# One language-model layer: norm chains in another order, values 68 columns wide, moments from the accumulator, gates by Tanh

## The reference, cut to what matters

```python
h = _L0_tok_ref(weight, x, end_ids)
h = h + attn(_layernorm(h))           # 8 heads of 16
#   xn = layernorm(input);  Q, K: one number per head;  V = xn @ Wv per head
#   P = softmax(-(Q - K)**2 / 4);  O = P @ V;  head_result @ Wm + input
h = h + ffn(_layernorm(h))            # 8 experts, 2 chosen per row
#   hh = layernorm(input) * g + b;  logits = hh @ w_r.T + b_r
#   topk_vals, topk_idx = top_k(logits, 2);  gates = softmax(topk_vals)
#   hid = gelu(hh @ W1[e] + b1[e]);  out = sum gate * (hid @ W2[e] + b2[e])
#   return input + out
```

## Time and profile before

| | us |
|---|---|
| median of three runs | 105.89 |
| the runs | 105.89, 107.15, 105.58 |
| profiled execution, its own time | 105.69 |
| its span, first to last instruction | 104.0 |
| busy in the span: PE, DVE, ACT, POOL | 85.4, 58.5, 55.4, 32.5 |

### The profile page before, as it was taken

How to read it: one execution, slowest core, us unless ns; L and a number is a source line. 1 busy time by engine, 2 the same in 40 slices (tenths; PEclk the granted TensorE clock), 3 DMA queues, 4 the chain that set the end, 5 groups by cost and what they waited for, 6 DMA issues and landing times.

```text
span 104.0 us, 1441 instructions
## 1 busy us (share of the span) xinstructions
PE 85.4 (82%) x435; PEld 67.6 (65%) x435; DVE 58.5 (56%) x174; ACT 55.4 (53%) x120; POOL 32.5 (31%) x65
## 2 busy tenths in 40 slices
PE   0081998499699995379999999999999999989940
PEld 0051437467499983369777777777777776779940
DVE  0998569688989555628809113404041329259870
ACT  0757814689998412213934564645556563118750
POOL 6963130039999624400000005415050505000000
PEclk9999999999999999955569999999999999999999
DMA  0589999090000000000000000000000000003774
GB/s 5 67 294 403 323 290 276 21 378 28 0 9 0 0 0 0 0 0 0 0 0 0 6 0 0 0 0 0 0 0 0 6 0 0 0 3 106 297 275 129
DMA packets 8168, 7.59 MB, mean 73 GB/s; under 512 B 1441, under 2 KB 6241, under 8 KB 8033
## 3 DMA queue, kind: packets, MB, share of 16 engines
q1 hardware_dynamic: 7440, 7.41, 22.5%
q10 hardware_dynamic: 720, 0.10, 0.6%
HBM read 5.40 MB, written 2.11 MB: 72 GB/s over the span
## 4 chain that ended last, share of the span: by engine, by line
PE 70%; DVE 15%; ACT 4%; issue 4%; DMA 3%; POOL 1%; DVEq 0%
PE ps L1214 20%; PE ps L1133 8%; PE ps L1299 7%; PE ps L1203 6%; PE ps L1204 6%; PE ps L1205 5%; PE ps L1047 4%; PE ps L1092 3%; DMA ends_i<-in_end_ids 3%; DVE closest L842 2%; PE ps L1226 1%; ACT hn_t L573 1%; PE ps L1107 1%; PE ps L1118 1%; ACT L638 1%
## 5 line engine op out<-in xcount | busy, mean ns | idle before, releaser
L657 ACT ACTIVATE w_f<-ps,ffn_cols 128x384 f32<-128x384 f32 x32 | 18.2, 580 | 15.9 <-PE ps L1205 15.9
L1214 PE MATMUL ps<-w_f 128*128 128x384 f32 x64 | 26.0, 496 | 0.0
L1203 PE MATMUL ps<-hn_hi,w_hi 128*128 128x384 f32 (+2 forms) x35 | 21.4, 613 | 1.4 <-DVE hn_lo L888 1.2
L513 POOL TENSOR_TENSOR acc<-acc,term 128x384 f32<-128x384 f32 x6 | 8.6, 1439 | 34.3 <-DVE term L973 34.3
L973 DVE SCALAR_TENSOR_TENSOR term<-ps,ffn_cols,gate_bc 128x384 f32<-128x384 f32 (+2 forms) x9 | 5.1, 571 | 22.8 <-PE ps L1214 15.9
L1204 PE MATMUL ps<-hn_lo,w_hi 128*128 128x384 f32 (+2 forms) x35 | 12.8, 366 | 0.0
L1205 PE MATMUL ps<-hn_hi,w_lo 128*128 128x384 f32 (+2 forms) x35 | 12.7, 364 | 0.0
L1214 PEld LDWEIGHTS ps<-w_f 128*128 128x128 f32 x64 | 11.8, 193 | 0.9
L1203 PEld LDWEIGHTS ps<-hn_hi,w_hi 128*128 128x128 f32 x35 | 7.8, 222 | 5.8 <-DVE hn_lo L888 1.3
L1204 PEld LDWEIGHTS ps<-hn_lo,w_hi 128*128 128x128 f32 x35 | 7.9, 227 | 3.8 <-issue 0.3
L461 POOL TENSOR_TENSOR w_lo<-w_f,w_hi 128x512 fp32r<-128x512 f32 x8 | 10.0, 1276 | 0.0
(11 more groups left out here) (185 smaller groups left out, 134.1 us busy)
## 6 DMA issues: line engine op xcount, KB each, us to landing
w_f<-in_w SPq DMA_DIRECT2D x4, 512.0 KB, 7.0
w_f<-in_w SPq DMA_DIRECT2D x8, 256.0 KB, 6.9
out_y<-w_f SPq DMA_DIRECT2D x6, 256.0 KB, 2.6
cls_all<-cls_dram SPq DMA_DIRECT2D x1, 1024.0 KB, 4.3
out_y<-w_f SPq DMA_DIRECT2D x4, 128.0 KB, 2.3
wm_sb<-in_wm ACTq DMA_DIRECT2D x1, 64.0 KB, 2.4
emb<-in_weight SPq DMA_DIRECT2D x1, 32.0 KB, 2.8
ffn_cols<-in_ffn_columns ACTq DMA_DIRECT2D x1, 24.0 KB, 5.2
```

The lines of the kernel that those rows point to most:

```text
L513: G.tensor_tensor(acc[:], acc[:], term[:, e % 2], ALU.add).then_inc(acc_ready, 1)
L657: nc.scalar.activation(hid[:, e % 2, f], ps[:, n % 4, 0:ROWS], ACT.Gelu, bias=b1_col[:, e, f:f + 1]).then_inc(gelu_ready, 1)
L1203: M(dst, w1_hi[:, e, c], hn_hi[:, rows], start=True, stop=False)
L1214: M(ps[:, 4 + e % 2, 0:ROWS], w2_f[:, e, f], hid[:, e % 2, f], start=(f == 0), stop=(f == FT - 1)).then_inc(down_done, 1)
```

## The change

It does six things.

1. `v_cnt` has 68 columns instead of 128, and the products stream 68. The zeros, and the waits for them, go.
2. DVE takes the moments from PSUM, where the accumulated row lies, and no longer from ACT's copy. The copy waits for the moments' read, `double_norm` waits for the copy.
3. The order of the chains changes on DVE, ACT and PE.
4. The Gelu table is loaded behind the last exponential of the attention.
5. The two gates are 0.5 + 0.5 tanh(half the difference of the two chosen logits): ACT's Tanh stands ahead of the fourth Gelu. The row maximum, the exponential, the sum and the reciprocal go.
6. `down(0, 0)` waits until the logits are read.

```diff
-        v_cnt = sb("v_cnt", [P, STATES, PAIRS, P])
+        v_cnt = sb("v_cnt", [P, STATES, PAIRS, B * VB])
...
-                pool.wait_ge(value_zero, 1)
...
-            nc.scalar.activation(v_cnt[:, :, :, B * VB:P].rearrange("p s k n -> p (s k) n"),
-                                 ident[:, 0:P - B * VB].unsqueeze(1).to_broadcast([P, STATES * PAIRS, P - B * VB]),
-                                 ACT.Copy, scale=0.0).then_inc(value_zero, 1)
...
             def take_residual(i):
-                act.wait_ge(att_done, i + 1)
+                act.wait_ge(mean_read, i + 1)
...
             exps(2, 0)
+            turn_heads(0)
             exps(2, 1)
-            turn_heads(0)
             exps(2, 2)
             exps(2, 3)
+
+            nc.scalar.activation(warm2[:], iota_part[:], ACT.Gelu)
             take_residual(0)
             turn_heads(1)
             take_rows(0)
+            turn_heads(2)
             take_residual(1)
-            turn_heads(2)
             take_rows(1)
             take_residual(2)
             take_rows(2)
 
-            act.wait_ge(shifted_ready, 1)
-            nc.scalar.activation(e_exp[:], shifted[:], ACT.Exp).then_inc(gexp_ready, 1)
-
-            nc.scalar.activation(warm2[:], iota_part[:], ACT.Gelu)
...
+                    if n == 3:
+
+                        act.wait_ge(gap_ready, 1)
+                        nc.scalar.activation(pair_tanh[:], pair_gap[:], ACT.Tanh).then_inc(tanh_ready, 1)
...
                 dve.wait_ge(att_done, i + 1)
-                dve.wait_ge(h1_ready, i + 1)
-                moments(h1[:, i], i, stats3, mv3)
+                V.bn_stats(stats3[:, i], ps[:, att_bank(i), 3 * P:4 * P]).then_inc(mean_read, 1)
+                dve.wait_ge(mean_read, i + 1)
+                step(V.bn_aggr(mv3[:, i], stats3[:, i]))
+                settle()
...
                 dve.wait_ge(rstd3_ready, 2 * i + 1)
+                dve.wait_ge(h1_ready, i + 1)
                 V.tensor_scalar(hn[:, i], h1[:, i], mv3[:, i, 0:1], rstd3[:, i, 1:2], ALU.subtract, ALU.mult).then_inc(hn_ready, 1)
...
+            normalise_heads(1)
             dve.wait_ge(small_in, 16 * SMALL)
             residual(0)
-            normalise_heads(1)
+            normalise_heads(2)
             double_norm(0)
-            normalise_heads(2)
             residual(1)
...
-            step(V.tensor_reduce(top[:, :, 0], logit[:], AX.X, ALU.max))
-            settle()
-            V.tensor_tensor(shifted[:], logit[:], top[:].to_broadcast([P, NT, E]), ALU.subtract).then_inc(shifted_ready, 1)
...
-            dve.wait_ge(gexp_ready, 1)
-            step(V.scalar_tensor_tensor(out=chosen[:], in0=rank[:], scalar=2.0, in1=e_exp[:], op0=ALU.is_lt,
+            step(V.scalar_tensor_tensor(out=pair_logit[:], in0=rank[:], scalar=2.0, in1=logit[:], op0=ALU.is_lt,
                                         op1=ALU.mult))
-            settle()
-            step(V.tensor_reduce(gsum[:, :, 0], chosen[:], AX.X, ALU.add))
-            settle()
-            step(V.reciprocal(grec[:], gsum[:]))
-            settle()
+            step(V.tensor_scalar(pair_half[:], rank[:], 2.0, 0.5, ALU.is_lt, ALU.mult))
+            settle()
+            step(V.tensor_reduce(pair_sum[:, :, 0], pair_logit[:], AX.X, ALU.add))
+            settle()
+            V.scalar_tensor_tensor(out=pair_gap[:], in0=pair_sum[:].to_broadcast([P, NT, E]), scalar=-0.5, in1=logit[:],
+                                   op0=ALU.mult, op1=ALU.add).then_inc(gap_ready, 1)
+            dve.wait_ge(tanh_ready, 1)
             dve.wait_ge(gate_zero, 1)
...
+            step(V.scalar_tensor_tensor(out=pair_half[:], in0=pair_tanh[:], scalar=1.0, in1=pair_half[:], op0=ALU.add, op1=ALU.mult))
+            settle()
+            V.tensor_copy(gate[:, :, 0:2 * LOW].rearrange("p t (g e) -> p t g e", e=LOW)[:, :, :, 0:E],
+                          pair_half[:].unsqueeze(2).to_broadcast(twice)).then_inc(gate_ready, 1)
...
             weighted(1, 2)
+            weighted(1, 3)
             output(0)
-            weighted(1, 3)
-            weighted(2, 0)
-            weighted(2, 1)
-            weighted(2, 2)
+            for k in range(PAIRS):
+                weighted(2, k)
             turn_back(1)
-            weighted(2, 3)
             output(1)
+            turn_back(2)
             turn_rows(0)
-            turn_back(2)
             route(0)
...
+                    if e == 0:
+
+                        pe.wait_ge(logit_read, NT)
```

More of the change, by code:

```diff
@@ L187, in build @@
         rank = sb("rank", [P, NT, E])
[L188 to L193, removed]
+        pair_half = sb("pair_half", [P, NT, E])
+        pair_logit = sb("pair_logit", [P, NT, E])
+        pair_sum = sb("pair_sum", [P, NT, 1])
+        pair_gap = sb("pair_gap", [P, NT, E])
+        pair_tanh = sb("pair_tanh", [P, NT, E])
         gate = sb("gate", [P, NT, P])
@@ L247, in build @@
         query_split = sem("query_split")
-        value_zero = sem("value_zero")
         xb_ready = sem("xb_ready")
@@ L286, in build @@
         h1_ready = sem("h1_ready")
+        mean_read = sem("mean_read")
         base_ready = sem("base_ready")
@@ L295, in build @@
         logit_read = sem("logit_read")
-        shifted_ready = sem("shifted_ready")
-        gexp_ready = sem("gexp_ready")
+        gap_ready = sem("gap_ready")
+        tanh_ready = sem("tanh_ready")
         gate_zero = sem("gate_zero")
@@ L734, in _ @@
                                  ALU.mult, ALU.add).then_inc(carry_ready, 1)
-            def moments(src, i, st, m):
-                step(V.bn_stats(st[:, i], src))
-                settle()
-                step(V.bn_aggr(m[:, i], st[:, i]))
-                settle()
             dve.wait_ge(h0_ready, 1)
@@ L951, in _ @@
             settle()
-            dve.wait_ge(gexp_ready, 1)
-            step(V.scalar_tensor_tensor(out=chosen[:], in0=rank[:], scalar=2.0, in1=e_exp[:], op0=ALU.is_lt,
+            step(V.scalar_tensor_tensor(out=pair_logit[:], in0=rank[:], scalar=2.0, in1=logit[:], op0=ALU.is_lt,
                                         op1=ALU.mult))
+            step(V.tensor_scalar(pair_half[:], rank[:], 2.0, 0.5, ALU.is_lt, ALU.mult))
             settle()
-            step(V.tensor_reduce(gsum[:, :, 0], chosen[:], AX.X, ALU.add))
+            step(V.tensor_reduce(pair_sum[:, :, 0], pair_logit[:], AX.X, ALU.add))
             settle()
-            step(V.reciprocal(grec[:], gsum[:]))
-            settle()
+            V.scalar_tensor_tensor(out=pair_gap[:], in0=pair_sum[:].to_broadcast([P, NT, E]), scalar=-0.5, in1=logit[:],
+                                   op0=ALU.mult, op1=ALU.add).then_inc(gap_ready, 1)
+            dve.wait_ge(tanh_ready, 1)
             dve.wait_ge(gate_zero, 1)
             twice = [P, NT, 2, E]
-            V.tensor_tensor(gate[:, :, 0:2 * LOW].rearrange("p t (g e) -> p t g e", e=LOW)[:, :, :, 0:E], chosen[:].unsqueeze(2).to_broadcast(twice),
-                            grec[:].unsqueeze(3).to_broadcast(twice), ALU.mult).then_inc(gate_ready, 1)
+            step(V.scalar_tensor_tensor(out=pair_half[:], in0=pair_tanh[:], scalar=1.0, in1=pair_half[:], op0=ALU.add, op1=ALU.mult))
+            settle()
+            V.tensor_copy(gate[:, :, 0:2 * LOW].rearrange("p t (g e) -> p t g e", e=LOW)[:, :, :, 0:E],
+                          pair_half[:].unsqueeze(2).to_broadcast(twice)).then_inc(gate_ready, 1)
             def weigh(e, rows=slice(0, ROWS)):
@@ L1132, in weighted @@
                 for st in range(STATES):
-                    mm = M(ps[:, O_BANKS[i % 2], k * P:(k + 1) * P], prob[:, k, st, tile(i)], v_cnt[:, st, k],
+                    mm = M(ps[:, O_BANKS[i % 2], k * P:k * P + B * VB], prob[:, k, st, tile(i)], v_cnt[:, st, k],
                            start=(st == 0), stop=(st == STATES - 1))
```

## The result

| | us |
|---|---|
| changed kernel, median of four runs | 102.92 (102.75 to 104.17) |
| kernel before, beside it | 106.14 (105.58 to 107.15) |
| ratio | 0.974, 95% interval 0.968 to 0.979 |
| profiled execution, changed kernel: time, span | 104.17, 102.5 |

The kernel is faster by 2.6%. Its time lies in the forecast's range, but it is the price of the first rival (102.9), not of the forecast (100.6). Ten runs of the changed kernel were made in all, in two sittings: 102.75, 102.84, 103.0, 104.17, and 103.9, 103.97, 104.26, 104.69, 100.09 and 100.11. The last two are the only ones whose mean granted clock was 0.999 or 1.0; the other eight had 0.94 to 0.97, and five of these eight took longer than the range's 103.5. Ratios compare, on each side, the runs within 1.5% of the fastest.

What follows compares the result with a forecast made beforehand. TensorE was taken as the bound from the first FFN matmul (43.70 us), at half clock until 53.94, behind a serial chain. Chain 1.45, early rows 1.1 and late rows 2.8 take 105.69 to 100.35, forecast 100.6 us, range 99.5 to 103.5.

Steps and rivals of the forecast that it cites:

- first rival: Ahead of the FFN: the clock falls anyway near 43.7 us; 102.9 us, or 102.2 if it returns sooner; chance 0.26.
- the clock is the assumption: Stretch ahead of 43.70 us: busy about two thirds of its time instead of 0.72 of 3.36 us, so the clock stays full.
- a stretch at half: Sign in the changed profile: if the granted clock shows a stretch at half again, the prediction is wrong.
- The sum on top of that assumption: Whole kernel: down(0,1) starts near 49.2 us instead of 54.57, a gain of 5.35; 105.69 - 5.35 = 100.35 us.
- its other case: The clock falls already before the early rows, which lose their 1.0 us again: 103.9 us; chance 0.06.
- The chain: Serial hops between engines, heads to split, for three row tiles: first FFN matmul at 42.25 us instead of 43.70, gain 1.45.
- rival 5: Chain before the FFN: the order gains nothing, another hop ends last, FFN starts at 43.7 us as now; 105 us; chance 0.02.
- Values 68 wide: The 72 value passes on TensorE: narrower columns booked at 0, bounds 0 to 3.8 us, since 128 and 256 columns agree.
- rival 2: Value products: narrow ones are quicker after all, 0.06 us a pass; about 1.2 us earlier, 99.4 us; chance 0.05.
- The table load: ScalarE, behind the last exponential at 34.80 us: the 1.28 us load ends near 36.3, covered by value products, cost 0.
- rival 3: Gates: Tanh costs two more table loads, TensorE's stall grows by 1.28 us; 101.9 us; chance 0.03.
- Rival 4: Value products, about 33.5 us: the clock falls inside them, some 37 passes at 0.21 instead of 0.11; 108.4 us; chance 0.04.

## Why the prediction was right and wrong

- **The step that failed** is the one named "the clock is the assumption": that a stretch "busy for about two thirds of its time" would not end in a fall. It was busy for 2.20 of 3.40 us, as foretold, and in the profile the clock fell at its end; so it did in the other profile, and six more of the ten runs have a mean clock (0.94 to 0.97) that tells of a fall but not of its place. With the gaps filled (3.35 of 3.40) it did not fall there; all ten runs of the two kernels timed with such fillers (100.74 and 100.35 us) had a mean clock of 0.986 or more. By the forecast's own sign, a stretch at half, it was wrong. I gave the case 0.54; the evidence I had was one fall after 0.72 us of work and one tail without a fall, and nothing in between. The tail was no good evidence: in the changed kernel's profile the clock falls in it.
- **The sum on top of that assumption was right.** The two runs with a full clock took 100.09 and 100.11 us against 100.35 reckoned from the profiled execution. In the profile with fillers down(0,1) starts 20.28 us after the first value product (49.42 - 29.14), before 25.80 (54.41 - 28.61): 5.5 us earlier, where 5.35 were reckoned.
- **Rival 1 was right in its cause, and lucky in its number.** It gave 102.9 for a fall near 43.7 that spares the early rows, and the first four runs have a median of 102.92. But both profiles show the fall at 42.4 and 42.0 us, ahead of the first FFN product; that is its other case, priced at 103.9, and these executions took 104.17 and 103.9. The runs at 102.75 to 103.0 have mean clocks of 0.949 to 0.966, and no profile shows one. As an estimate, 0.966 over its 101.0 us would be 6.9 us at half instead of 10.24. The median of all ten runs is 103.45, which lies just inside the range.
- **The chain**: a gain of 1.45 us was reckoned, 1.56 measured (15.09 to 13.53). So rival 5 fell. The shares were not told apart, and the new order, counted on as part of the gain, costs time. Step by step: the moments from PSUM alone give 1.80 (13.29), narrow values with the load and the gates 0.05 (13.24), and the new order takes 0.29 back (13.53). What was wrong with the order is not double_norm(0): it was written off behind TensorE's queue until 38.8 us, and counted from the first value product TensorE came to it at just that time (39.27 - 0.46). It is turn_back(1) behind all value products, which the reckoning had right in time (output(1) to end at 38.95; measured 39.34 - 0.46 = 38.88) but did not compare with the old place. The bound of 0.2 us more for moments on PSUM came from no row; measured were 0.30 against 0.29. With fillers the old order gains 0.15 us (13.37 against 13.52).
- **Values 68 wide**: booked at 0, measured 0.13 us over the chain in the new order. The rows of equal pace at 128 and 256 columns were read rightly, and rival 2 fell (0.110 us a pass, not 0.06). "TensorE: Matmul & The Clock Gate" of the Trainium skill has in its section "LDWEIGHTS (loading the stationary operand)" a load time that goes by the columns of the weights; worked out for 128 it is an estimate of 107 ns. The 0.110 us a pass of these products at full clock agrees with it, the 0.21 us at half clock does not.
- **The table load**: cost 0 under the value products, right (35.28 to 36.56, with nothing waiting). Its place is worth nothing either; what is worth something, once the clock is up, is that no Exp follows: 2.9 us in one run of each, of which 1.5 is the wait and the rest mostly the clock (a fall that need not come with the wait).
- **Tanh** costs no further load: rival 3 fell. The Trainium skill ("ScalarE: Activation LUTs", section "Table sets: the hidden batching unit") lists tanh with other sets than gelu's. Read as the whole list, it would ask for a load at Tanh; the trace does not agree: Tanh runs between Gelus in 0.22 us, with no load. Its wait ahead of the gates' transposes, put at 0.8, was 0.31 us on TensorE's row with the clock held and nothing with it down.
- **Rival 4** (a fall inside the narrow products) did not happen in any profile: every fall shown lies at 41.4 us or later, behind them.

## What to carry to other kernels

Where a serial chain over four engines feeds a dense stage, ask two things apart: when the stage starts, and at which clock; the second can be worth as much as the first, and here cheap products in TensorE's waits bought it in most kernels (in the kernel before, in two runs of four). A reduction that can read the accumulator should not queue behind another engine's copy of it: while the clock fell, that one edit did what all six did together. An edit that takes an engine off the path pays more once TensorE runs fast enough to wait for that engine (0.24 us of wait for the first Gelu at half clock, 1.50 at full), so test such edits again after the clock is held. And ask of the chain of waits, not of the instruction that came later, what a new order costs.

## What was not expected of the hardware

The same program kept its full clock in 2 of 10 runs and lost it in the others (10.24 us at half in both of its profiles), 100.1 against 102.75 to 104.7 us. After a wait of 1.50 us in the midst of dense work one profile has a fall of 3.42 us, another, with the same wait at the same place, has none. Nor does the busy share alone tell the cases apart: TensorE was busy for 1.90 us from 46.00 to 49.40 in the kernel before with fillers, and kept its clock; it was busy for 2.54 us from 38.00 to 41.40 in the kernel before with moments from PSUM, and lost it at 41.40. What decides it stays open.
